# Two sets of gather slots and index copies one tile ahead in the first edge stage of a graph kernel

## The reference

```python
# layer 0
msg = edge_weight[:, None] * x[src]
agg = segment_sum(msg, dst, num_segments=N)
x1  = layernorm(x + relu((x + agg) @ W1 + b1) @ W2 + b2)
# layer 1
h1  = x1 @ lin1_w.T
f   = softplus(edge_attr @ nn_w1.T + nn_b1) - LOG2      # the hidden layer of the filter
W   = (softplus(f @ nn_w2.T + nn_b2) - LOG2) * c[:, None]
agg = segment_sum(W * h1[edge_index[1]], edge_index[0], num_segments=N)
out = layernorm(x1 + (h1 + agg) @ lin2_w.T + lin2_b)
```

## Time and profile before

| | |
|---|---|
| median of 3 runs | 8999.62 us (8995.32 to 9006.65) |
| the profiled execution, its own time | 9018.67 us |
| its span in the trace | 9016.8 us |
| busy: PE, DVE, ACT, POOL | 66%, 65%, 38%, 69% |
| first and last gather of layer 0 (L499) start | 72.3 us, 4331.1 us |
| first and last scatter of layer 1 (L1317) start | 4533.8 us, 8625.5 us |

### The profile page before, as it was taken

How to read it: one execution, slowest core, us unless ns; L and a number is a source line. 1 busy time by engine, 2 the same in 40 slices (tenths; PEclk the granted TensorE clock), 3 DMA queues, 4 the chain that set the end, 5 groups by cost and what they waited for, 6 DMA issues and landing times. The chain is left out here.

```text
span 9016.8 us, 199238 instructions
## 1 busy us (share of the span) xinstructions
PE 5937.2 (66%) x35386; PEld 4768.7 (53%) x35658; DVE 5857.1 (65%) x17865; ACT 3463.0 (38%) x6782; POOL 6200.3 (69%) x6552
## 2 busy tenths in 40 slices
PE   4666666666666666666655555767666676676687
PEld 3444444444444444444444444666666666666676
DVE  6666666666666665555655555777777777777776
ACT  3333333333333333333544443344434443334302
POOL 5777767777777767777167777777777777777720
PEclk7777767667677766676855556888888888888897
DMA  5444444444444444444444445666666666666676
GB/s 155 145 146 144 146 140 146 145 146 145 144 146 146 144 141 147 144 147 144 145 136 135 133 133 156 216 213 214 213 212 217 213 213 214 212 212 215 213 238 206
DMA packets 805241, 1537.36 MB, mean 171 GB/s; under 512 B 193150, under 2 KB 206900, under 8 KB 804707
## 3 DMA queue, kind: packets, MB, share of 16 engines
q1 hardware_dynamic: 595415, 1097.64, 37.8%
q0 software_dynamic: 209456, 436.16, 16.5%
q10 hardware_dynamic: 348, 3.33, 0.1%
HBM read 971.97 MB, written 564.58 MB: 170 GB/s over the span
## 5 line engine op out<-in xcount | busy, mean ns | idle before, releaser
L499 POOL DMA_INDIRECT xg<-x_rows,gidx x3224 | 3046.0, 945 | 1266.1 <-issue 925.8
L1317 POOL DMA_INDIRECT sorted_messages<-rows,sidx x3224 | 3110.6, 965 | 1156.0 <-issue 947.4
L551 PE MATMUL bank<-onehot,xg 128*128 128x42 f32 x6448 | 1106.2, 324 | 1409.7 <-DMA xg<-x_rows,gidx 1399.9
L551 PEld LDWEIGHTS bank<-onehot,xg 128*128 128x128 f32 x6448 | 993.2, 230 | 1483.4 <-DMA xg<-x_rows,gidx 1471.5
L561 PE MATMUL bank<-attr,nn 128*128 128x512 f32 x1612 | 1459.8, 1060 | 1.2 <-DVE hid L585 0.8
L1245 PE MATMUL bank<-hot,block_rows 128*128 128x128 f32 x8256 | 1388.9, 344 | 32.4 <-DVE hot L1399 32.3
L1245 PEld LDWEIGHTS bank<-hot,block_rows 128*128 128x128 f32 x8256 | 1341.1, 257 | 58.4 <-issue 20.3
L1215 PE MATMUL bank<-w_nn2T,e_hid 128*128 128x128 f32 x6448 | 1042.1, 314 | 308.9 <-DMA e_hid<-hidden 301.1
L1215 PEld LDWEIGHTS bank<-w_nn2T,e_hid 128*128 128x128 f32 x6448 | 1008.9, 226 | 265.8 <-DMA e_hid<-hidden 233.1
L1226 PE MATMUL bank<-h1w,ohT 128*128 128x128 bf16 x3224 | 333.1, 266 | 970.4 <-DVE ohT L1346 970.4
L1370 DVE SCALAR_TENSOR_TENSOR rows<-filt,meta,bank 128x128 f32<-128x128 f32 x3224 | 904.8, 343 | 103.5 <-DVE filt L1361 68.5
(11 more groups left out here) (220 smaller groups left out, 7860.8 us busy)
## 6 DMA issues: line engine op xcount, KB each, us to landing
block_rows<-sorted_messages SPq DMA_DIRECT2D x346, 792.0 KB
hidden<-hid SPq DMA_DIRECT2D x404, 512.0 KB
e_hid<-hidden SPq DMA_DIRECT2D x403, 512.0 KB
sorted_messages<-zero SPq DMA_DIRECT2D x403, 264.0 KB
dstb<-dst SPq DMA_DIRECT2D x403, 256.0 KB
attr<-attr_cols SPq DMA_DIRECT2D x403, 204.0 KB
xg<-x_rows,gidx POOLq DMA_INDIRECT x3224
sorted_messages<-rows,sidx POOLq DMA_INDIRECT x3224
```

The source lines that it names most:

```text
L499: pool.indirect_dma_start(xg[s][:, :], None, x_rows, bass.IndirectOffsetOnAxis(ap=gidx[s // HALF][:, s % HALF:s % HALF + 1], axis=0),).the ...
L551: nc.tensor.matmul(bank[0][:, 0:WIN], xg[s][:, :], onehot[:, s, :], start=(s == 0), stop=(s == SUB - 1)).then_inc(summed, 1)
L1317: pool.indirect_dma_start(table, bass.IndirectOffsetOnAxis(ap=sidx[b][h][:, s:s + 1], axis=0), rows[b][h][:, s, :], None).then_inc(landed[ ...
```

## The change

The slots are doubled to sixteen (xg[b][s], b = 0 for even and 1 for odd tiles), the two index tiles become four (gidx[b][h]), and the semaphores `gathered` and `summed` are split by b. All four loops over tiles are written with `in_pairs`. A gather of tile t+1 now waits for the use of its slot by tile t-1. ACT copies the indices of tile t+1 ahead of the softplus of tile t, and once per tile, not once per window. DVE waits for both `summed` counters. The setup primes eight more semaphores with small DMAs from POOL.

```diff
@@ -116,7 +116,7 @@
         bank = [ctx.enter_context(nc.psum_tensor(f"bank{i}", [P, 512], f32)) for i in range(8)]
         aggT = sb("aggT", [D, NPAD + P], f32)
         x_loaded = sem("x_loaded")
-        gathered = [sem(f"gathered{s}") for s in range(SUB)]
+        gathered = [[sem(f"gathered{b}_{s}") for s in range(SUB)] for b in range(2)]
         landed = [[sem(f"landed{k}_{h}") for h in range(2)] for k in range(2)]
 
 
...
@@ -218,7 +218,8 @@
                     pool.memset(half_pi[:, :], PI / 2).then_inc(s_pool, 1)
                     pool.wait_ge(s_pool, 1)
                     for s in range(SUB):
-                        prime(pool, spare[s:s + 1, :], gathered[s], zero)
+                        prime(pool, spare[s:s + 1, :], gathered[0][s], zero)
+                        prime(pool, spare[32 + s:33 + s, :], gathered[1][s], zero)
                     pool.memset(ident[:, :], 0.0).then_inc(s_pool, 1)
                     pool.memset(lower[:, :], 1.0).then_inc(s_pool, 1)
                     pool.memset(ones16[:, :], 1.0).then_inc(s_pool, 1)
...
@@ -370,8 +372,8 @@
                 def sb2(name, shape, dt):
                     return c2.enter_context(nc.sbuf_tensor(name, shape, dt))
 
-                gidx = [sb2(f"gidx{h}", [P, HALF], i32) for h in range(2)]
-                xg = [sb2(f"xg{s}", [P, D], f32) for s in range(SUB)]
+                gidx = [[sb2(f"gidx{b}_{h}", [P, HALF], i32) for h in range(2)] for b in range(2)]
+                xg = [[sb2(f"xg{b}_{s}", [P, D], f32) for s in range(SUB)] for b in range(2)]
                 onehot = sb2("onehot", [P, SUB, WIN], f32)
                 rel = sb2("rel", [P, SUB], f32)
                 oha = sb2("oha", [P, SUB, NB], bf16)
@@ -389,7 +391,8 @@
                 turns_f = sb2("turns_f", [P, 2], f32)
                 weights_in = sem("weights_in")
                 gidx_ready = [sem(f"gidx_ready{h}") for h in range(2)]
-                summed, onehot_ready, fixed_set = sem("summed"), sem("onehot_ready"), sem("fixed_set")
+                summed = [sem(f"gathers_summed{b}") for b in range(2)]
+                onehot_ready, fixed_set = sem("onehot_ready"), sem("fixed_set")
                 flushed, rel_set, passed, passed_sp = sem("flushed"), sem("rel_set"), sem("passed_pool"), sem("passed_sp")
                 oha_set, counted, ahead_set, seen_set, pair_set, count_set, rank_set = (
                     sem(n) for n in ("oha_set", "counted", "ahead_set", "seen_set", "pair_set", "count_set", "rank_set"))
@@ -467,40 +470,56 @@
 
                         nc.scalar.preload_act_table_set("natural_log_exp_and_others")
                         jobs = TileTable(act, "act0", nwin)
-                        with act.Fori(0, T) as t:
+                        sent = RowTable(act, "act0")
+
+                        def copy_indices(t, b):
+
+                            for h in range(2):
+                                for s in range(HALF * h, HALF * h + HALF):
+                                    act.wait_ge(gathered[b][s], 16 * (sent.number(b) + 1))
+                                nc.scalar.activation(gidx[b][h][:, :], srci[:, ds(t * SUB + HALF * h, HALF)],
+                                                     ACT.Copy).then_inc(gidx_ready[h], 1)
+
+                        def softplus_1(t, b):
                             windows = jobs.windows()
-                            with act.Fori(0, windows):
-                                j = jobs.number()
-                                jobs.read_ahead(t)
-                                for h in range(2):
-                                    for s in range(HALF * h, HALF * h + HALF):
-                                        act.wait_ge(gathered[s], 16 * (j + 1))
-                                    nc.scalar.activation(gidx[h][:, :], srci[:, ds(t * SUB + HALF * h, HALF)],
-                                                         ACT.Copy).then_inc(gidx_ready[h], 1)
-                                jobs.step()
+                            jobs.read_ahead(t)
                             for h in range(2):
                                 soft_1(t, h)
+                            with act.Fori(0, windows):
+                                sent.step(b)
+
+                        def tile(t, b):
+                            copy_indices(t + 1, 1 - b)
+                            softplus_1(t, b)
+
+                        copy_indices(0, 0)
+                        in_pairs(act, 0, T - 1, tile)
+                        softplus_1(T - 1, (T - 1) % 2)
                         for h in range(2):
                             soft_1(T, h)
 
                     @block.gpsimd
                     def _(pool):
                         jobs = TileTable(pool, "pool0", nwin)
-                        with pool.Fori(0, T) as t:
+                        sent = RowTable(pool, "pool0")
+
+                        def tile(t, b):
                             windows = jobs.windows()
                             with pool.Fori(0, windows):
-                                j = jobs.number()
+                                n = sent.number(b)
                                 for s in range(SUB):
                                     if s == HALF + 1:
                                         jobs.read_ahead(t)
                                     if s % HALF == 0:
-                                        pool.wait_ge(gidx_ready[s // HALF], j + 1)
-                                    wait_apart(pool, summed, SUB * j + s + 1, passed)
+                                        pool.wait_ge(gidx_ready[s // HALF], t + 1)
+                                    wait_apart(pool, summed[b], SUB * n + s + 1, passed)
                                     pool.indirect_dma_start(
-                                        xg[s][:, :], None, x_rows,
-                                        bass.IndirectOffsetOnAxis(ap=gidx[s // HALF][:, s % HALF:s % HALF + 1], axis=0),
-                                    ).then_inc(gathered[s], 16)
-                                jobs.step()
+                                        xg[b][s][:, :], None, x_rows,
+                                        bass.IndirectOffsetOnAxis(ap=gidx[b][s // HALF][:, s % HALF:s % HALF + 1], axis=0),
+                                    ).then_inc(gathered[b][s], 16)
+                                sent.step(b)
+
+                        in_pairs(pool, 0, T, tile)
 
                     @block.tensor
                     def _(pe):
...
 
-                        nc.tensor.matmul(bank[0][:, 0:WIN], lower[:, :], zero16[:, 0:WIN], start=True, stop=True).then_inc(summed, SUB)
+                        nc.tensor.matmul(bank[0][:, 0:WIN], lower[:, :], zero16[:, 0:WIN], start=True, stop=True).then_inc(summed[0], SUB)
+                        pe.sem_inc(summed[1], SUB)
...
@@ -547,10 +569,11 @@
                                     for s in range(SUB):
                                         if s == HALF:
                                             jobs.read_ahead(t)
-                                        pe.wait_ge(gathered[s], 16 * (j + 2))
-                                        nc.tensor.matmul(bank[0][:, 0:WIN], xg[s][:, :], onehot[:, s, :],
-                                                         start=(s == 0), stop=(s == SUB - 1)).then_inc(summed, 1)
+                                        pe.wait_ge(gathered[b][s], 16 * (sent.number(b) + 2))
+                                        nc.tensor.matmul(bank[0][:, 0:WIN], xg[b][s][:, :], onehot[:, s, :],
+                                                         start=(s == 0), stop=(s == SUB - 1)).then_inc(summed[b], 1)
                                     jobs.step()
+                                    sent.step(b)
                                 if q + 1 < PARTS:
                                     pe.wait_ge(digits_set, t * 2 + 2)
                                     nc.tensor.matmul(digit_counts, high[:, :, :].rearrange("p s u -> p (s u)"), low[:, :, :].rearrange("p s v -> p (s v)"),
@@ -559,6 +582,8 @@
                                     pe.wait_ge(attr_in, 16 * (t + 1))
                                     pe.wait_ge(hid_set, taken_up(t, h))
                                     nc.tensor.matmul(bank[2 + h][:, :], nn1[:, :], attr[:, h, :], start=True, stop=True).then_inc(z1_set, 1)
+
+                            in_pairs(pe, first, past_last, tile)
 
                     @block.vector
                     def _(dve):
...
+                        sent = RowTable(dve, "dve0")
                         last = dve.alloc_register("dve0_last_node")
                         dve.reg_mov(last, 0)
+
+                        def all_summed():
+
+                            for b in range(2):
+                                dve.wait_ge(summed[b], SUB * (sent.number(b) + 1))
+
                         for q, first, past_last in parts:
                             plan_part(q)
-                            with dve.Fori(first, past_last) as t:
+
```

(7 more changed lines are left out.)

11 lines of the change are left out of this document (7 added, 4 removed).

## The result

| | before | changed |
|---|---|---|
| median of 4 runs each, taken beside each other | 8997.47 us (8982.64 to 9006.65) | 8774.16 us (8771.18 to 8796.3) |
| ratio | | 0.9759, 95% interval 0.9738 to 0.9779 |
| the profiled execution, its span | 9018.67 us, 9016.8 us | 8796.30 us, 8794.7 us |
| layer 0, first to last gather | 4258.8 us | 4033.2 us |
| layer 1, first to last scatter | 4091.7 us | 4096.2 us |

The account below looks back on a forecast made before the run. Layer 0 was taken as bound by POOL's issue rate plus a handshake of POOL, PE and ACT with one tile of slots. 231.7 us saved less 4 gave 228, so 8999.6 - 228 = 8772 us; range 8750 to 8850.

Parts of the forecast that it names:

- The step: POOL's time from gather to gather in layer 0: 1.2495 us, 10.0 us a tile, 231.7 us less than 4258.8.
- Starts: 4 us taken back from the saving for layer 0's very start, the starts of parts and loop entries.
- What held POOL: POOL's waits in layer 0: 288 for slots PE had not freed, 181.3 us; 212 for indices, 159.1 us.
- Rooms: Slack before POOL is held up: ACT's copies 6.2 us after landing, 9.3 through the softplus; slots cover a 6.9 us delay.
- The PE and DVE ring: Loop between PE and DVE in layer 0 that no slot shortens: closes in 7.9 to 9.0 us, under 10.0.
- The rival with 10.3 us a tile: PE and DVE's ring takes over in layer 0: 402 tiles lose 0.3 us each, 121 us, 8893 us; chance 0.08.
- PE's wait for gathers: Expected sign in layer 0: PE's waiting for gathered rows falls from 3.5 to about 2.9 us a tile.
- The longer DMA instruction: Rival: POOL's gathers take 1.025 us beside DVE's work, no change, 9011 us; chance 0.07 together with no effect.
- Loop branches: Rival: jumps of longer loop bodies slow DVE, 281 us more, 9280 us; decides from 2.5 us a tile; slower 0.05.
- Scaling: The saving in the profiled execution, 9018.67 to 8791 us, carries over to the median: 8999.6 - 228 = 8772 us.

## Why the prediction was right

**The step.** 1.2495 us was forecast from layer 1's gap and layer 0's own duration, and 1.2514 measured. The layer's span was 4027.1 + 4 = 4031 in the forecast, and it is 4033.2. 228 us were to be saved; 225.6 were in layer 0, and 223.3 between the medians.

**Starts.** Four us were taken back for the starts and loop entries. The stalls are gone as said. That the 4 us lie there was not shown: gathers are 1 ns longer (4.4 us in all), which alone would do, so that this term fits is luck.

**What held POOL.** The prediction split the lost time between slots (288 waits, 181.3 us) and indices (212, 159.1 us) by the names in the earlier trace rows. 307 of these 500 are the normal gap. The copy held POOL in 292 tiles and the slots in four, as said above. The sum did not use the split, so it stands.

**Rooms.** Their sizes were off in both directions. The landing of a tile's last gather was taken as 3.0 us and is a median of 4.4 in the changed kernel (3.0 before, same measure). It holds up ACT's second copy only, which the fifth gather needs, 5 us after the first: the prediction had it wanted with the first. Measured as the time by which a copy is done before POOL needs it, the second copy has a median of 9.5 us and never under 4.5. The first copy has a median of 7.7, where 9.3 were forecast. Behind the starts of parts both this room and that of slot 0 run down: the first copy comes with none to spare in tiles 3, 105 and 205 (counted from 0), and slot 0 with 0.5 us in tile 204 (0.1 on the other chip). So the starts of parts cost nothing, as forecast, but only just. ACT's timeline in an undisturbed tile: the first copy comes straight behind the softplus, the second waits for a landing, and then ACT waits for PE.

```profile
2004.09 0.20 ACT L480 ACTIVATE gidx<-srci 128x4 int32 x1
2006.90 0.20 ACT L480 ACTIVATE gidx<-srci 128x4 int32 x1 [2.60 <-DMA xg<-x_rows,gidx]
2010.33 0.60 ACT L465 ACTIVATE soft<-bank 128x512 f32<-128x512 f32 x1 [3.23 <-PE bank L584]
```

With 2.2 us more on ACT the period stayed at 10.0.

**The PE and DVE ring.** Forecast 7.9 to 9.0, with 1.0 us of room. It closes within 8.76 us (seven gathers, two attr tiles). The granted clock of 0.71 that the prediction names for its rows is that of 1900 to 2125 us, a stretch ahead of them; those from 2235 to 2257 us have 0.75. The rival with 10.3 us a tile did not come; it took half a product more to get there, with `attr` late as well.

**Missed.** The ring over `attr`. Just behind the start PE waits for it tile after tile:

```profile
93.73 3.77 PE L584 MATMUL bank<-attr,nn 128*128 128x512 f32 x4 [1.03 <-DMA attr<-attr_cols]
103.54 3.78 PE L584 MATMUL bank<-attr,nn 128*128 128x512 f32 x4 [0.78 <-DMA attr<-attr_cols]
```

The first eight such products follow each other in 9.3 to 9.8 us, where PE has to catch up, so the ring has 0.2 to 0.7 us of room, less than the one that the prediction weighed. That it did no harm is luck; what a slower load would have cost was not tried.

**PE's wait for gathers.** Forecast 3.5 to 2.9 us a tile, measured 838.1 / 403 = 2.1 (on the other chip 3.3 to 2.6). The missing 0.9 us are in PE's other waits, which hardly existed before: 181.6 us for `attr` and 173.8 for DVE's digits (L718). The three together are 1193.5 / 403 = 2.96 us a tile.

**The longer DMA instruction.** 946 against 945 ns, with DVE busy for 145.22 of 225 us, more than in the earlier trace rows:

```profile
1900.00:2125.00 225.00, 154.31 (x825) 101.44 (x823) 145.22 (x364) 87.78 (x176) 169.98 (x181) 0.68 0.48 148
```

The Trainium skill's rule of the shared port ("SBUF — State Buffer", section "SBUF: two separate sides") would let a DVE instruction in a two-port mode hold up the gathers' descriptors. No run here shows that for DVE's instructions of this layer.

**Loop branches.** DVE's gap for "issue" at L698 is 499.4 / 403 = 1.24 us, against 1.06: 0.18 us more, far from the 2.5 that decide. The Trainium skill ("Runtime: NRT & Kernel Launch", section "Instruction fetch mechanics") would have no change for a body of this size. What the 0.18 us are was not looked for; the wait and the register instruction that were added could be it.

**Scaling.** The difference of the profiled executions (222.4 us) did carry over to the medians (223.3). On another chip the difference is 163.9 us, since before is faster on it. The forecast time would be as close there (8783.54), the forecast gain would not.

## What to carry to other kernels

When an engine runs within a few per cent of its own issue rate, look for all the handshakes that hold it: a second buffer set and an earlier index copy gave 0.1% and 0.6% alone and 1.8% together on like chips. To see which one comes last, measure the time from each possible releaser's end to the start of the waiting instruction, tile by tile; the true one stands at a constant distance (0.885 us here for the copy, 0.81 for the slot), whatever name the profile gives. The floor is the busy time plus the gap that stays with no wait in between; forecast from it, and then close every ring that remains, those over single-buffered loads on other queues too. A gain can differ by half a per cent from chip to chip (1.8% and 2.4% here).

## What was not expected of the hardware

- The gap of 0.30 us between POOL's gathers is there with and without waits and counting between them: 0.945 + 0.30 us a gather. A scatter, with them, takes 0.965 + 0.30.
- When a gather lands goes with what is sent beside it. Where SP sent its load of `attr` between 1.5 us before a gather's start and 1.5 us after its end, the gather landed in a median of 3.7 us before and 3.8 in the changed kernel, the others in 2.4 and 2.5. `attr` is sent 6.8 us behind a tile's first gather before and 8.8 us behind it in the changed kernel, so the slow gathers were the sixth and seventh (3.9 and 4.0 us) and are now the eighth and the next first (4.4 and 3.9). That the load is the cause fits (the slow places move with it in the other traces with eight gathers too) and was not tested by itself. The mean of all landings went from 2.6 to 2.8 us only.
- Two chips differ by 0.3 to 0.4 us in the landing of a tile's last gather and hardly in POOL's rate (10.01 and 9.99 us a tile).
- Half a product more in each tile raised the granted clock from 0.70 to 0.79 and cut the product's mean from 1075 to 939 ns, so the added work cost less than its count.
